# A graph layer's max over edges: the second list's words laid out by ScalarE, its running sum counted in place, and the chain's steps placed anew

## What is computed

```
h = maximum(layernorm(x), 0)
feat = concatenate([h[dst], h[src] - h[dst]])
msg = feat @ W.T + b
out = x + segment_max(msg, dst)
```

## Time and profile before

| | us |
|---|---|
| runs | 876.09, 879.14, 879.84 (median 879.14) |
| profiled execution: its own time | 878.57 |
| its span, first to last instruction | 876.9 |
| busy: DVE | 801.8 (91%) |
| busy: POOL | 619.9 (71%) |
| busy: PE | 547.9 (62%) |
| busy: ACT | 408.1 (47%) |

### The profile page before, as it was taken

The page is one execution under the profiler, slowest core; times in us unless marked ns, Lnnn a source line. Parts: engine busy times, 40 slices in busy tenths (PEclk is TensorE's granted clock), DMA queues, the critical chain, the costliest instruction groups (busy, mean ns, idle before and its releaser), DMA issues.

```text
span 876.9 us, 8002 instructions
## 1 busy us (share of the span) xinstructions
PE 547.9 (62%) x2442; PEld 264.7 (30%) x2442; DVE 801.8 (91%) x1290; ACT 408.1 (47%) x244; POOL 619.9 (71%) x631
## 2 busy tenths in 40 slices
PE   2564896000000468777777767788888888888852
PEld 1553565000000123322233323333333333333331
DVE  7989999999999799998899899999999998888985
ACT  3786213000039055775675769755555756351000
POOL 2677277887777767777777777777777677777742
PEclk9999999555555599998899888999999999999985
DMA  8951003323364665665554556555656654453655
GB/s 261 204 150 25 8 21 94 90 59 92 86 194 97 182 194 174 175 171 137 174 157 149 171 138 175 173 179 170 185 172 193 217 193 150 148 176 79 95 108 166
DMA packets 114694, 126.75 MB, mean 145 GB/s; under 512 B 19542, under 2 KB 96836, under 8 KB 114379
## 3 DMA queue, kind: packets, MB, share of 16 engines
q1 hardware_dynamic: 95090, 86.33, 32.3%
q0 software_dynamic: 19376, 38.94, 18.6%
q10 hardware_dynamic: 184, 0.96, 0.3%
HBM read 86.43 MB, written 40.57 MB: 145 GB/s over the span
## 4 chain that ended last, share of the span: by engine, by line
DVE 33%; PE 17%; issue 13%; DMA 1%; ACT 1%; POOL 0%; DVEq 0%; POOLq 0%; SPq 0%
DVE acc L1291 19%; PE ps L852 17%; DVE maxima L1235 10%; DVE hT L1244 2%; DVE hT L1258 1%; DMA ohs<-winners 1%; ACT ohs L598 1%; DVE hT L1249 1%; DVE hT L1349 1%; DMA hT<-running_max,end_row 0%; DMA running_max<-maxima 0%; POOL hT L705 0%; POOLq L197 0%; DVEq L1290 0%; DVE hT L1351 0%
## 5 line engine op out<-in xcount | busy, mean ns | idle before, releaser
L726 POOL DMA_INDIRECT rows<-near_table,idx x503 | 516.5, 1027 | 181.2 <-issue 134.6
L1291 DVE TENSOR_TENSOR acc<-ps,acc 128x1924 f32<-128x1924 f32 x196 | 344.1, 1780 | 34.7 <-PE ps L852 34.4
L852 PE MATMUL ps<-ohs,near 128*128 128x481 fp8e3 x1404 | 319.3, 381 | 77.4 <-DVE acc L1291 68.9
L598 ACT ACTIVATE ohs<-ohs,spike 128x6272 fp8e3<-128x6272 uint8 x36 | 197.8, 5513 | 82.3 <-DMA ohs<-winners 82.3
L852 PEld LDWEIGHTS ps<-ohs,near 128*128 128x128 bf16 x1404 | 134.2, 100 | 262.5 <-DVE acc L1291 88.9
L1235 DVE SCALAR_TENSOR_TENSOR maxima<-maxima,fresh,rows 128x128 f32<-128x128 f32 x503 | 176.4, 351 | 13.7
L593 ACT ACTIVATE hT<-k,off 128x1600 bf16<-128x1600 int16 (+6 forms) x49 | 65.9, 1392 | 205.8 <-DVE hT L1249 182.8
L852 PE MATMUL ps<-sorts_mem,near 128*128 128x481 fp8e3 x507 | 117.7, 387 | 28.6 <-DVE acc L1291 26.7
L840 PE MATMUL ps<-flags,ones 128*128 128x10 f32 x2 | 0.6, 360 | 150.3 <-DVE spare L1269 150.3
L598 ACT ACTIVATE sorts_mem<-sorts_mem,spike 128x6272 fp8e3<-128x6272 uint8 x13 | 71.7, 5515 | 23.2 <-DMA sorts_mem<-winners 23.2
L852 PEld LDWEIGHTS ps<-sorts_mem,near 128*128 128x128 bf16 x507 | 49.4, 102 | 96.6 <-DVE acc L1291 31.1
(11 more groups left out here) (182 smaller groups left out, 461.7 us busy)
## 6 DMA issues: line engine op xcount, KB each, us to landing
running_max<-maxima SPq DMA_DIRECT2D x63, 512.0 KB, 3.7
ohs<-winners SPq DMA_DIRECT2D x36, 784.0 KB, 6.5
sorts_mem<-winners SPq DMA_DIRECT2D x13, 784.0 KB, 6.5
rows<-near_table,idx POOLq DMA_INDIRECT x503, 3.2
acc<-in_x SPq DMA_DIRECT2D x6, 512.0 KB, 7.2
near_table<-acc SPq DMA_DIRECT2D x12, 256.0 KB, 4.5
base<-in_x SPq DMA_DIRECT2D x1, 2744.0 KB
out_x<-hT SPq DMA_DIRECT2D x12, 224.0 KB
```

Of the source, the lines that this page charges most:

```text
L598: nc.scalar.activation(oh[t % OHS], oh_bytes[t % OHS], ACT.Abs_reciprocal_sqrt, bias=spike[:, 0:1], scale=float(SPIKE), saturate=False).th ...
L726: nc.gpsimd.indirect_dma_start(rows[:, n % (SLOTS * GATHERS), :], None, near_table[:, :], bass.IndirectOffsetOnAxis(idx[:, n:n + 1], 0)).t ...
L852: last = nc.tensor.matmul(bank(4 * (n % 2) + c - UNITS[r][0])[:, 0:CHUNK], near[:, t, part, :], oh[t % OHS][:, at:at + CHUNK], start=part ...
L1291: V.tensor_tensor(into, found[:, 0:z - a, 0:CHUNK], into, ALU.max).then_inc(max_done, 1)
```

## The change

**The second list's words** (h = 1 alone; the first list's code is the same work, now called `first_words`):

- ACT writes the numbers: for each of the 34 tiles one ACTIVATE over 64 slots reads the sorted numbers with a step of 50 int16 and adds j * 2^14 + 8192 from a new tile `j_bias`, into `words[1][1]`. It starts when the sort's result is there (`k2_ready`).
- DVE multiplies the loser flags with "not a double" in place in int16 (one instruction of 2176), in slot-major order. ACT turns them to tile-major and to f32 in one ACTIVATE of 2176 as 2^20 - 2^20 * flag ("stays"; semaphores `losers_known`, `stays_ready`).
- The running sum now adds up 2^20 for each slot that is not a loser, starting at -2^31, with int32 output: it is the distance already shifted by 20, in place. The instructions for position less sum and for the shift are gone, and so is the part of `iot16` that they read.
- DVE takes the loser bit out of the numbers where a slot stays (L1183 of the new kernel, both inputs contiguous), and joins number and distance as before.

**The order.** The table's costs for flags and words are new (23.3 us become 14.6), and a gather is now taken to cost 1.26 us during a round (before 1.3) and 1.3 us during a tree (before 1.4). So `schedule()` places other steps: 492 (before 484) come ahead of the rest steps, and 12 places are left for the rest (before 20).

**The end.** A fourth cut `(47, 496)`: the finals of tiles 44 to 46 wait for 62 blocks of 8, those of 47 and 48 alone for all 63. PE's transposes use all eight banks.

```diff
-CUTS = ((36, 400), (44, 472), (49, 504))
+CUTS = ((36, 400), (44, 472), (47, 496), (49, 504))
...
-    pieces += [("flags", cost, 1.8) for cost in (2.05, 2.6, 2.5, 2.5, 3.9, 0.1)]
-    pieces += [("words", cost, 1.8) for cost in (5.0, 4.2, 5.3, 2.05, 3.0)]
+    pieces += [("flags", cost, 1.8) for cost in (2.05, 2.6, 2.5, 2.5, 1.4)]
+    pieces += [("words", cost, 1.8) for cost in (6.0, 3.0, 1.2, 3.0)]
...
-            pieces += [("round", (2.15, 1.65, 1.65, 1.65)[r], 1.3)]
+            pieces += [("round", (2.15, 1.65, 1.65, 1.65)[r], 1.26)]
         if trees < 25:
-            pieces += [(name, cost, 1.4) for name, cost in tree_pieces(trees)]
+            pieces += [(name, cost, 1.3) for name, cost in tree_pieces(trees)]
...
+            a, z, _ = PARTS[1]
+            numbers, at = words[1][1], LEFT + (z - a) * KS
+            act.wait_ge(k2_ready, 1)
+            for j in range(a, z):
+                last = nc.scalar.activation(numbers[:, LEFT + (j - a) * KS:LEFT + (j - a + 1) * KS], S1[:, :, j], ACT.Identity,
+                                            bias=j_bias[:, j:j + 1])
+            last.then_inc(numbers_ready, 1)
+            act.wait_ge(losers_known, 1)
+            nc.scalar.activation(picks[1][:, LEFT:at].rearrange("p (j k) -> p j k", k=KS),
+                                 loser_bits.rearrange("p k j -> p j k"), ACT.Identity, bias=one_step[:, 0:1],
+                                 scale=-float(1 << SHIFT_AT)).then_inc(stays_ready, 1)
...
-            stored(CUTS[1][1] // STEPS)
-            for g in range(early_groups, waiting_groups):
-                finals(g)
-            stored(all_blocks)
-            for g in range(waiting_groups, groups):
-                finals(g)
+            for (a, _), (z, cap) in zip(CUTS, CUTS[1:]):
+                stored(cap // STEPS)
+                finals(a, z)
...
-                if g >= 4:
-                    pe.wait_ge(joined, g - 3)
+                if g >= 8:
+                    pe.wait_ge(joined, g - 7)
...
+                if h:
+                    V.tensor_tensor(loser_bits, loser_bits, ne[:, :, 0:real], ALU.mult).then_inc(losers_known, 1)
+                    yield
+                    return
...
+            def second_words():
...
+                then(V.tensor_scalar(stays[:, 0:LEFT], left_real_sb[:, :], -step, step, ALU.mult, ALU.add))
+                then(V.tensor_copy(numbers[:, 0:LEFT], left_sb[:, :]))
+                then(V.tensor_scalar(cnt[:, 0:n], iota_f[:, 1:n + 1], float(KS), LEFT - 2048.0, ALU.mult, ALU.add))
+                dve.wait_ge(stays_ready, 1)
+                settled()
+                then(V.tensor_tensor_scan(shift, stays, lowest[:, 0:1].to_broadcast([P, at]), -2.0 ** 31, ALU.add, ALU.max))
+                yield
+                dve.wait_ge(numbers_ready, 1)
+                settled()
+                for u, v in in_parts(LEFT, at):
+                    then(V.scalar_tensor_tensor(numbers[:, u:v], stays[:, u:v], -float(IS_LOSER) / step, numbers[:, u:v],
+                                                ALU.mult, ALU.add))
+                then(V.scalar_tensor_tensor(tot[:, 1:n + 1], shift[:, LEFT + KS - 1:at:KS], -1.0 / step, cnt[:, 0:n],
+                                            ALU.mult, ALU.add))
+                then(V.tensor_scalar(tot[:, 0:1], shift[:, LEFT - 1:LEFT], -1.0 / step, LEFT - 2048.0, ALU.mult, ALU.add))
+                yield
...
                 for u, v in in_parts(0, at):
-                    then(V.tensor_tensor(words[h][0][:, u:v], words[h][0][:, u:v], words[h][1][:, u:v], ALU.bitwise_or))
+                    then(V.tensor_tensor(word[:, u:v], numbers[:, u:v], shift[:, u:v], ALU.bitwise_or))
```

More of the change, by code:

```diff
@@ L226, in edgeconv @@
         var = sb("var", [P, tiles], F32)
+        j_bias = sb("j_bias", [P, tiles], F32)
+        lowest = sb("lowest", [P, 1], F32)
+        one_step = sb("one_step", [P, 1], F32)
         std = sb("std", [P, tiles], F32)
@@ L309, in edgeconv @@
         count_ps = bank(7)[:, 256:257]
[L310 removed]
+        flag_ps = bank(7)[:, 0:11]
         x_pad_set = sem("x_pad_set")
@@ L733, in _ @@
                         stored(CUTS[0][1] // STEPS)
-                    finals(g)
+                    finals(*spans[g])
                 if (b + 1) * GATHERS == decide_at:
@@ L883, in _ @@
             then(V.memset(eps[:, :], EPS))
+            then(V.memset(lowest[:, :], -2.0 ** 32))
+            then(V.memset(one_step[:, :], float(1 << SHIFT_AT)))
             then(V.memset(flags[:, :], 0.0))
@@ L983, in _ @@
             then(V.memset(run_at(0), LOW))
+            then(V.tensor_scalar(j_bias[:, :], iota_f[:, 0:tiles], float(1 << J_AT), float(IS_LOSER), ALU.mult, ALU.add))
             settled()
@@ L1125, in loser_words @@
                                                 ALU.mult, ALU.add))
-                yield
                 settled()
                 for u, v in in_parts(0, at):
-                    then(V.scalar_tensor_tensor(words[h][1][:, u:v], r[:, u:v], -1.0, iot16[:, u:v], ALU.mult, ALU.add))
+                    then(V.scalar_tensor_tensor(words[0][1][:, u:v], r[:, u:v], -1.0, iot16[:, u:v], ALU.mult, ALU.add))
                 for u, v in in_parts(0, n, MOST_AT_ONCE // KS):
@@ L1132, in loser_words @@
                                                 ALU.mult, ALU.add))
-                then(V.tensor_copy(tot[:, 1:n + 1], r[:, before + KS - 1:at:KS]))
-                if h:
-                    then(V.tensor_copy(tot[:, 0:1], r[:, before - 1:before]))
-                else:
-                    then(V.memset(tot[:, 0:1], 0.0))
+                then(V.tensor_copy(tot[:, 1:n + 1], r[:, KS - 1:at:KS]))
+                then(V.memset(tot[:, 0:1], 0.0))
+                settled()
+                for u, v in in_parts(0, at, 2 * MOST_AT_ONCE):
+                    then(V.tensor_scalar(words[0][1][:, u:v], words[0][1][:, u:v], SHIFT_AT, None, ALU.logical_shift_left))
@@ new lines, in first_words @@
+                then(V.tensor_tensor(has[:, 0:n], tot[:, 1:n + 1], tot[:, 0:n], ALU.is_gt))
+                then(V.tensor_scalar(flags[:, 4:5], tot[:, n:n + 1], float(FIRST_CAP - 1), None, ALU.is_gt))
+                then(V.tensor_scalar(end_f[:, a:z], tot[:, 1:n + 1], float(FIRST_CAP - 1), None, ALU.min))
+                then(V.tensor_scalar(left_count[:, :], tot[:, n:n + 1], float(PARTS[0][2]), None, ALU.subtract))
+                settled()
+                for u, v in in_parts(0, at):
+                    then(V.tensor_tensor(words[0][0][:, u:v], words[0][0][:, u:v], words[0][1][:, u:v], ALU.bitwise_or))
@@ new lines, in second_words @@
+                then(V.tensor_scalar(flags[:, 5:6], tot[:, n:n + 1], float(CT - first - 1), None, ALU.is_gt))
+                for c, (cut, most_steps) in enumerate(CUTS[:-1]):
+                    then(V.tensor_scalar(flags[:, 6 + c:7 + c], tot[:, cut - a:cut - a + 1], float(most_steps - first - 1), None,
+                                         ALU.is_gt))
+                for at_cut, (cut, most_steps) in zip([a] + [cut for cut, _ in CUTS], CUTS):
+                    then(V.tensor_scalar(end_f[:, at_cut:cut], tot[:, at_cut - a + 1:cut - a + 1], float(first),
+                                         float(most_steps - 1), ALU.add, ALU.min))
@@ L1297, in _ @@
                 pass
-            for _ in loser_words(0):
-                pass
+            first_words()
             for _ in compact(0):
```

83 lines of the change are left out of this document (39 added, 44 removed).

## The result

The kernel after took 863.7 us (median; 862.84 to 866.34) against 879.5 us (876.09 to 880.07) for the kernel before on the same chip: ratio 0.983, 95% interval 0.981 to 0.986. The forecast was 865.3 us, with a range of 861 to 871. The profiled execution took 863.67 us with a span of 862.0, so by the traces the gain is 14.9 us.

A forecast was written before the change was run, and what follows sets the result against it. DVE was taken to bound the kernel. From the profiled 878.57 us, words -9.5, tail -4.9 and SP with row waits +1.1 sum to -13.3, giving 865.3 us; range for 8 in 10: 861 to 871.

The forecast's parts named there:

- The words: Second list's words on DVE, ahead of the rounds: work removed and added gives -9.5 us (-8.5 to -9.9).
- the new wait: DVE waiting for ACT's stays before the running sum: 0.7 us taken, bounds 0.3 and 1.7.
- a sign of being wrong: Before the running sum: a DVE wait of over 2 us for ACT would show the forecast wrong.
- The upper bound: Wait for ACT before the running sum: 1.7 us if the stays take 3.4, the result 1 us later.
- The places of chain steps: 0.: Chain steps on DVE: each costs the same 0.35 us wherever it stands, so moving them cancels.
- The first rival: Rounds: steps put into DVE's waits for PE are free, up to 2.8 us back, 862.5 us; chance 0.14.
- The tail: Joins at the end: DVE's 4.91 us wait for a final gather goes, -4.9 us.
- SP and row waits: SP's stores at the end and short waits for rows here and there: +1.1 us, bounds 0 and 2.5.
- The second rival: Tree rounds and one-hot loads: gathers become the bound, DVE waits some 4.5 us, 869.8 us; chance 0.14.
- Condition (a): Whole program: DVE time saved ahead of the rounds counts fully if POOL's gathers, which do not move, land in time.
- the rival on the other side: Tree rounds: PE's clock stays at half, 2.7 us for each such tile, 892 us with ten; chance 0.03.
- The change acted: Opposite of a rival: joined tail as late as before, row waits eat half the rest, 874.5 us or more; chance 0.03.

The follow-up runs named there:

- e7: Changed kernel with ACT's stays read in order and written with a step of 64 f32, instead of read with a step: 863.9 us.
- e2: Changed kernel with the old cuts, banks and gather costs, and chain steps about where they stood before, so the new words alone: 873.5 us, ratio 0.994.
- e3: Changed kernel with only the table's two gather costs as before (1.3 and 1.4): 868.0 us, ratio 0.988.
- e1: Kernel before with the fourth cut, finals by tile and eight transpose banks; words and order stay: 876.2 us, ratio 0.996.
- e5: Changed kernel with ten writes of 0.92 us added on POOL, one ahead of each of gather blocks 50 to 59: 868.9 us, ratio 0.990.
- e6: Kernel before with ten writes of 0.92 us added on POOL, one ahead of each of gather blocks 50 to 59: 878.2 us, ratio 0.999.
- e9: Changed kernel with three blocks of gathers in flight instead of two: 860.1 us, ratio 0.979.
- e11: Kernel before with three blocks of gathers in flight instead of two: 878.1 us, ratio 1.000.
- the parts alone: Two runs, e1 (tail alone) and e2 (words alone): 2.4 and 5.1 us faster than the kernel before.
- e4: Changed kernel with the running sum made twice, 4.8 us more on DVE ahead of the rounds: 867.4 us, ratio 0.988.

## Why the prediction was right, and where not

The total was right within 1.6 us and the mechanism of both large terms held. That the error is so small is luck, because misses cancelled: the words gave 1.7 us less than forecast and the row waits took 2.5 more, while the waits for PE, put at nothing, gave 5.4.

- **The words: -9.5, measured -7.8.** The removed and added instructions came out as costed: product 1.33 (1.38), loser bit 2.62 (2.6), running sum 4.81 (4.81), numbers through at 181.2, ahead of the flags at 184.8. The step that failed is the new wait: 0.7 us taken, bounds 0.3 and 1.7, measured 2.49, which is over the 2 us that the prediction itself had named as a sign of being wrong. The stays took 4.15 us, over the 3.4 that DVE's ratio of strided to contiguous gave; ACT's own ratio is 1.9. e7 shows the same price on the write. The upper bound was the case for which the Trainium skill was quoted (SBUF — State Buffer, "Door 1": leaving the 16-byte line pays). The trace agrees with that rule, and the price was higher than DVE's. The first round was met (291.2, forecast 291.5), with the 2.0 us of shorter PE wait making up for the ACT wait.
- **"The places of chain steps: 0."** This was the term that was wrong in kind. It was argued that a step costs 0.35 us wherever it stands. It doesn't: in a PE wait it is free, ahead of its row it costs a wait, and behind the last round it delays the last gather. e2 and e3 price the three: 3.7 us of row wait that the new order avoids, 3.5 us of PE waits and 4 us at the tail. The first rival, PE's waits swallowing steps, was given 0.14 and up to 2.8 us; by the waits it is 34.4 - 29.0 = 5.4 us. It had the place wrong, though. It pointed first to the last stretch of rounds, where the waits stayed at 11.8 us: the block of four more in the last 12 tiles stands behind the last round. And 2.0 us of the 5.4 came at the very first max, which the rival did not name.
- **The tail: -4.9, and it came (4.91 to 0.16).** The reasoning by cover, joins against landing, was right, but the credit belongs to cut and order together: the cut alone gives 3.6 us of it (e1), and without the order 4 us come back (e3).
- **SP and row waits: +1.1, bounds 0 and 2.5; measured 3.6 of row waits and almost nothing at SP.** SP's last issue ended at 859.2 where 860.2 was expected. The row waits stand between 522 and 702 us; the reserve had been laid out as least at gather 336, wanted at 589.4, so the stretch was right and the size too small. The second rival, gathers become the bound, was thus also partly true. That POOL's line had no reserve left is what e5 and e6, e9 and e11 show from both sides. Condition (a), POOL's gathers do not move, held to the end (835.34 and 835.33), but two things were overlooked in the trace of before: POOL does not always issue back to back (before 33 gathers it stood 14.9 us until a landing, up to 2.1 at a time where 0.3 is the usual gap; three blocks in flight remove that), and one gather stretches to 4.87 us beside DVE's running sum.
- **PE's clock** stayed at 0.90, 0.99 and 1.00 in the three stretches: the rival on the other side did not occur. The change acted.

Against the spans: words -7.8, PE waits -5.4, row waits +3.6, tail -4.8; these sum to -14.4 of 14.9.

## What to carry to other kernels

When a change speeds up one engine of a schedule that was written around arrival times, lay the old order over the new times before counting the gain: here the parts alone gave 7.5 of 15 us, and the other half came only with the order that fits. An engine that is 72% busy, as POOL is here, can have no reserve at all: look at the longest single wait of the issuing engine and at who ends it, and price it by adding work to that engine alone, in both kernels. Here that led to one number, three blocks of gathers in flight instead of two, which gives another 3.6 us after the change and none before it.

## What was not expected of the hardware

ACT takes 1.9 ns an element to turn 64x34 into 34x64 from int16 to f32 (4.15 us for 2176) and 1.8 with the step on the write, twice the 0.99 of the contiguous rows. A gather issued on POOL beside DVE's running sum takes 4.7 to 5.2 us instead of 0.94, in all 13 traces, and a second sum stretches a second gather (4.53 us, e4). For DVE's running sum, int32 output and a broadcast second input cost nothing (4.81 us as before). The 34 small ACTIVATEs of 64 elements filled 10.41 us, 0.31 each, where 0.36 was estimated.
